# A two-part transformer kernel on one core: clamp, Newton step and entry normalizing made by GpSimd in place of VectorE, with a new merge order

## The chip, the cores and the metric

The program runs on 1 core of one Trainium2 chip. The metric is the device time of one execution, in microseconds (us). Engines are named as the profile names them: PE is TensorE's matmul row and PEld its weight load, DVE is VectorE, ACT is ScalarE, POOL is GpSimd, SP is SyncE, which only issues transfers here.

## The reference, cut to what matters

`x` has 8 batches of 512 rows of 128 features. Each batch goes through a modulated layer norm, an attention with 16 heads of 8 features over all positions, a gated residual, a second modulated layer norm, two layers of a block with local attention, and a last gated residual.

```python
h = _layernorm(x) * (1 + ca) + sa
x = x + ga * attention(h)                  # 16 heads
h = _layernorm(x) * (1 + cb) + sb
x = x + gb * block(h)                      # 2 layers of _layer

def _layer(x, ...):
    q, k, v = split(shift_token(x) @ wqkv)  # 8 heads of 64
    q, k = l2norm(q) * qs, l2norm(k) * ksc  # t / max(norm(t), 1e-12)
    q, k = rotary_xpos(q, k)
    x = x + local_attention(q, k, v) @ wo   # windows of 64, looking one back
    h = layernorm(shift_token(x)) * lg + lb
    a, g = split(h @ w1 + b1)
    return x + (a * gelu(g)) @ w2 + b2
```

## The kernel before, in words

The work is cut into four streams of steps. Stream `a` is the first attention of all 8 batches, one after another. Streams `x`, `y` and `z` are the two-layer block: stream `x` takes batches 0, 1, 2 and 5, `y` takes 3 and 6, `z` takes 4 and 7 (`BATCHES`). Stream `x` runs beside `a`; `y` and `z` begin when `a` is over, because they use its memory. Each engine has a generator for each stream that issues one step at a time, and `merge` takes the steps in the order of a string of letters that is written out for each engine (`ORDER`). A second string, `BANKS`, says which PSUM bank each step of PE writes. Engines run their queue strictly in this order and wait for one another by semaphores, so an instruction that waits holds all that stands behind it on its engine.

One stream and layer of the block ("a stream layer", 16 in all) goes like this. PE projects keys, values and queries of 4 row tiles. For each of the 8 tiles of keys and queries ACT squares (L970), DVE multiplies by the rotary tables (L1258, L1262) and sums the squares over each head (L1266), and POOL adds the two rotary products (L825). When the 4 key tiles are summed, and again for the 4 query tiles, the norm is made from sums of 128x32: DVE clamps and shifts them (`b_norm`, L1272), ACT takes logarithm and exponential (L978, L980) for a first inverse root, DVE improves it with a Newton step of three instructions (`b_rnorm`, which calls `newton`, L1148 to L1150), and POOL multiplies the four tiles by it (`b_scale`, L833). Then PE transposes (L530), and for each of 8 heads come scores (L541, L548), maximum on DVE (L1284), exponential on ACT (L998), reciprocal on DVE (L1289), weighing on POOL (`b_probs`, L838), transpose (L558) and product with the values (L569). The output projection (L579), a layer norm and a gated hidden layer (L598, L604) close the layer.

The rows that enter an attention are normalized by DVE. For the first attention `a_normalize` does a Newton step on 128x4 numbers and four `tensor_scalar` of 128x128 into `xn` (L1154). For each batch that enters the block `b_enter_normalize` does the same into `xn2`, which is memory of `rot_work`. PE then transposes them (L442, L516). The layer norm inside the block reads PSUM, is written to `work`, and is not touched by the change.

In the first attention, DVE takes a maximum (L1191), ACT an exponential (L905), DVE a reciprocal (L1195) and POOL weighs the queries (`a_weigh`, L803) for each of 16 groups of a batch. POOL also splits keys and values into two parts (`a_split`, L786, L788) and adds the residual (`a_residual`, L792).

Of the kernel before, what the change touches and what calls it, by code (L numbers as in the profile page):

```python
# [14 lines left out]
P = 128  # L15
# [50 lines left out]
B_CHAIN = LN_CHAIN + (2 * 2 + LN_CHAIN) * L  # L66
# [4 lines left out]
        "aaaaaaaaaaaaaaaaaaaaaaaaaaaaaaaaaaaaaaaaaaaaaaaaaaaaaaaaaaaaaaaaaaaaaaaaaaaaaaxaaaaaaaaaaaaaaaaaaaaa"  # L71
        "aaaaaaaaaaxaaxxxxxxaxaaxxaaaaaaaxxaaaaxxxxaaaaaaaaaaaaaaaxxxxaaaaaaaaaaaaaaaaaaaaaaaaaaaaaaaaaaaaaaa"
        "aaaaaaaaaaaaaaaaaaaaaaaaaaaaxxaaaxaaxaaaaaaaaaaaaaaaaaaaaaaaaaaaaaxxxaxaxxaaaxxaaaxaaaaxxaaaaaaxaaax"
        "aaaaaaxaaaaxaxaxaaaxxxxxaaaaaaxaaaaaxxaaxxxxaxxaxaaaaaaaaaaxxaaxxxaxaaaaaaaaaxxaxxaaaaxxaaaxxxxaxxxa"
        "aaxxxaaaxxxaaaaxaxaaaxaaaaaxxxxaaxaxaxaaxaaaaaaxaaaaaaaaaaaaaaxaaaxxxaxxxxxaaaaaxxaaaaaaaaaaaxaxaxxx"
        "xaaaaaaaaaxxxaaxaaaaxxaaaxxaaaxxxaxxaxxxaxxxxxyxyyyyyyyxyyxxxxxxyxyyxxxxxxxxxxyyyyxxxxxxyyyyxyxxxyxx"
        "yyyxxyxxxxxyxyxxyyxxxyyxxyyyxyyxxxxxxyxxyxyyyyyyxzyzzzzzzzzzzxxxxxxzzxxzzzzxxyyyyyyyyzzzzyzxxxxxxyzz"
        "zzzzzzxxxzzxzyyzzzxzxzxxxzxyxyyxxyzxxzzxzzzzxyzxxyzxzzxzzxzzzzzyyxyxxxxxxzzxzzzzyyxxxxxyxzzxyyyzxzxx"
        "zyyyyxxzzyyxyxxxyzzzyzzzyzzzxyxxxzzzxzxzyxxxzyyyyyyzxxyzzyzxxxzxzzyzyyzxxyxxyyyyxyzxzzzxzzyyzzzzxzxx"
        "xxxxyyxyyxyyzzzzzzxxxxzxzxzzxzyzyyyxxzyxzxyzzzyyzzxxzzyzyyxzzxzxyyzyyxzyyxyzyxxyxyzxzzzyxxzzzxzxyxxy"  # L80
        "xxzzzzzzzzyyxxxyyyxzxxyxzxyzzxzyzzzyyyyxyyyxxyxxzxxzzzxzzyyyyyyzxxxzxzzxxxzxyxyxyzzyyzzxxzyxxxxyyzyy"
        "yzxyxyxxyyzxxzyzxyyxxxxyzxyxyxxzyxzzzzzzyxxxyyxyxyyxyzyxzyxxxxxxxx"
    ),
    "DVE": (
        "aaaaaaaaaaaaaaaaaaaaaaaaaaaaaaaaaaaaaaaaaaaaaaaaaaaaaaaaaaaaaaaaaaaxaaaaaaxaaaaaaaaaaaaaaxaaaaaaaaaa"
        "aaaaaaaaaaaaaaxaaaxaaaxaaxxaxxaaaxaaaxaaaxaaaaaaaxaxaaaaaxaaaaaaaaaaaaaaaaaaaaaaaaaaaaaaaaaaaaaaaaaa"
        "aaaaaaaaaaaaaaaaaaaaaaaaaaxxaxxxxaaaaxaaaaaaaaaaaaaaaaaaaaaaaaaaaaaaxxxxaxxxaaaxxxaaaxaaaaaxaaaaaaax"
        "aaaxaxaaaaaxaxaaaaaaaaxxxxaaaxaaaaaaaxaxaaxaxaaxaxaaaaaxxaaaxaaxaaaxaaaxaaaaaaxaaaaxxaaaxxxxaxxxaaxx"
        "xxaxxxxaaaxxaaaxaaxxaaxaaxaaaaaxaxaaxaaxaaaaaaxaaaaaxaaaaaxaaaaxaaaxaaxxaaaaxaxaaxaaaaxxaaaaaaaxxaxa"
        "aaxaaaaaaxaaaaaxxaxxaaxxxaaaxxaxxxxxxxxaxyxyxxxyxyxyyyyyxxxyyxxyxxxxxxxxyxyyxxxyyyxyyxxyyyxxxxyxyxxx"  # L90
        "xxxxyyyxxxyyxxyyyxyxxyxyxyyxxyxyxxxzyxzyyxzyyzzzzzzzzxxzzxzxzxxxxyzyzzxzyyzzzxzyxyzzxyzzzyzzzzzxzyzx"
        "zxxxxxxzzxzxxxzxxxyyxxxyxzzzzzxzxzxxxzxzyzzzzxxxyzxyxyzyzyyyzxxxyxyyxzyyxzzxyzxyyyyxzzzyyzxxzzxyzzzz"
        "zyyzzzyzxzxxzyxxxxzxzxzxzyyyxxxyyyxxyzzzxxxyzxyzzxyzxyzyxyxzxzxyyzzyxxxzzxzzxxzxzyxzyzxyxyxzzzzzyzzx"
        "yxxyzyyzyyzzzxxyzzzzzyzxyzyyyzyyxzxyyyxyzzyzyxzyyxxxyxxxzzzyxzzxxxxxxxzzzzzxxxyyyxzxyyxzzxxyxzxzyzyz"
        "yxyyxxzyyxzzxzzyzzyzxyxzzyxzxzxxzzyzxxyyzzyzyyyxxyxyyxzyyzyyyxyyxxyzxxxxyzzxyxxxxxzyxzxyyxxxyxyzzzxx"
        "xxyyxyxzyzyxxxxx"
    ),
    "ACT": (
        "aaaaaaaaaaaaaaaaaaaaaaaaaaaaaaaaaaaaaaaaaaaaaaaaaaxaaaaaaxaaaaaaaaaaaaaaaaaaxaaxaaaxxxaxxxxaaxaxxaaa"
        "axxaaaxxxaaaaaxxaaaaxxxxaaaaaaaaaaaaaaaaaaaaaaaaaaaaaaaaaaaaaaaaaaaaaxxaxaxxaaaxaaaaaaaaaaaaaaaaaaxx"  # L100
        "xaxxaaxxaaxaaxaxaaaaaaxaaaaxaxaaaaxaaxaaaaxaaaxxaxxxxxxaxaxaaaaxxaaxxxaaaaxxaaaxxaxxaaaaxxaxaxxxxxax"
        "xxaxaxxaxaxaaaaxaxaxaaxaaaaaaaaaaaaxaaaxaxaaxxaxxxaxxxaaxaxaxaaaaxaaxaxxxaaxxaaaaxaxaxxaaaxxxxxxaaaa"
        "xxxxxxxxxxyyxyyxyyyyyxyyyxyyyxyxxxxxxxxxyxxyyxxxyxyxyxxyyyxxyxxyyxxxyyxxxyyxxxxxyxyxxyyxxyyyxyyxxyxy"
        "yyxzxxzzyzzzzzzzzzzxzxxxzzxxzxzzxyyxzzyyxxzzzzyyxyxzzxxxyyyzzzzxxyzzzzxxzzxzzxyyzzxxxxzxxxzxyxxyyzxx"
        "yyxzxyzxxyzzzxzzzxzzzyyxzzxzzyzxzzyyzxxxxyyxyxzzxzyzyxzxyxxyzzyxxyyyzxyxxzzyzxxzzzzzyzxzzxxxzzyxxxyz"
        "xxxxzyzxxzxyxxyyxyyxyxxzyyyyyzzzxzzzzxyyyzzzxxzzyyzyyyzzzxzzxxzzxxxzyxzyxzzxyzyyyzxxzzxzyzyyxxyyyzzz"
        "zzxzxzzyyzyzyxxxyyxxyyzxyyxxzxzyxxzyxxxxzyxxxxxzzzzzzzzyxxxzxxyzzyxzzzyzxzyyyyxyyzzyxyzzzyzxzyyyzyzx"
        "yxxzzzxyyxzxxzxyxyzyzxyxzzxyyxxxxyyyyxzzyyyyzxxxxxyzyxxyyxxxyxzxyxxxzxyxzxxyzyxxyxxxx"
    ),
# [32 lines left out]
def build(nc, x, wmod, wqkv1, wqkv, wo, w1, w2, cols_in, rows_in_, rotary, out):  # L142
    with ExitStack() as ctx:
# [3 lines left out]
        def sb(name, shape, dt=F32):  # L147
            return tensor_in(ctx, name, shape, dt)
# [29 lines left out]
        clamp = sb("clamp", [P, J, H])  # L178
# [77 lines left out]
        def qk_of(s, i, w):  # L256
# [17 lines left out]
        s_gcol, s_tables, s_clamp, s_qz, s_kzero = (  # L274
            sem(n) for n in ("s_gcol", "s_tables", "s_clamp", "s_qz", "s_kzero"))
# [5 lines left out]
        xn_ready = sem("xn_ready")  # L281
# [15 lines left out]
        xn2_ready = sems("xn2_ready")  # L297
# [4 lines left out]
        ss_all, ss_log, ss_rsqrt, rn_ready = sems("ss_all"), sems("ss_log"), sems("ss_rsqrt"), sems("rn_ready")  # L302
# [460 lines left out]
        def _(pool):  # L763
# [17 lines left out]
            pool.memset(clamp[:], SHIFT2).then_inc(s_clamp, 1)  # L781
# [26 lines left out]
            def a_stream():  # L808
                for b in range(B):
                    for g in range(NG):  # L810
                        if b and g == 1:
                            a_residual(b - 1)
                            yield
                        a_weigh(b, g)
                        yield
                        if b + 1 < B and g in (5, 7):
                            a_split(b + 1, (g - 5) // 2)
                            yield
                a_residual(B - 1)
                yield  # L820
# [21 lines left out]
            def b_stream(s):  # L842
                for k in range(len(BATCHES[s])):
                    for l in range(L):
                        for n in range(2 * J):
                            if (k, l, n) == (0, 0, 0):
                                enter_wait(pool, s, k)
# [616 lines left out]
```

## Time and profile before

| | before |
|---|---|
| median of 3 runs | 1196.69 us (1193.58 to 1197.32) |
| profiled execution, its own time | 1196.15 us |
| span of the profiled execution | 1194.3 us |
| PE, DVE busy | 997.0 us (83%), 949.4 us (79%) |
| ACT, POOL busy | 918.2 us (77%), 508.1 us (43%) |
| mean granted clock of TensorE | 0.948 of full speed |

The span is the time from the first to the last instruction in the profile; 1.85 us of the execution's own time lie around it. Busy time leaves out waits for semaphores. The last step of the first attention begins at 559.7 us, so the run has two halves: up to about 560 us stream `a` beside stream `x`, then `x`, `y` and `z` together.

### The profile page before, as it was taken

Reading aid. Unit: us, or ns where it says so; the run is one execution under the profiler, and the core shown is the slowest. Engines: PE = TensorE matmul, PEld = TensorE weight load, DVE = VectorE, ACT = ScalarE, POOL = GpSimd, SP = SyncE. Lnnn points to the kernel's source line nnn. Section 1 sums busy time; section 2 is a strip of 40 time slices with the busy share of each in tenths; the row PEclk is TensorE's granted clock in tenths of the full one; section 3 lists DMA queues with packets and bytes.
Section 4 is the critical chain, followed back from the end, with each engine's and each line's share of the span. In section 5 each row is a group of like instructions: output and inputs, shape, how many; then the busy total and the mean of one; then the engine's idle time right before and its main releaser. Section 6 shows DMA issues by size and latency. Waiting matters only on the chain. (4 is left out here: it accounts for less than half of the span.)

```text
span 1194.3 us, 23996 instructions
## 1 busy us (share of the span) xinstructions
PE 997.0 (83%) x8124; PEld 510.0 (43%) x8124; DVE 949.4 (79%) x1947; ACT 918.2 (77%) x2782; POOL 508.1 (43%) x578
## 2 busy tenths in 40 slices
PE   2677787768888798778868897899999789999898
PEld 2232232223323352234336444655664357545664
DVE  4789898888869777986884699779769976789865
ACT  1698979899978988887659566868886587958983
POOL 5012143212105321343474058647823676348830
PEclk8699989999989898998989998999999999999999
DMA  5541305232204103001011001101110020001200
GB/s 206 180 142 36 106 1 146 62 107 71 72 0 130 43 28 115 10 10 24 1 31 34 10 1 32 33 1 32 33 41 10 10 63 16 18 1 32 46 20 27
DMA packets 28009, 59.18 MB, mean 50 GB/s; under 512 B 6192, under 2 KB 6384, under 8 KB 26736
## 3 DMA queue, kind: packets, MB, share of 16 engines
q1 hardware_dynamic: 27120, 56.33, 16.7%
q8 instruction: 67, 1.10, 0.4%
q10 hardware_dynamic: 768, 1.31, 0.3%
q14 instruction: 54, 0.44, 0.1%
HBM read 23.98 MB, written 18.87 MB: 36 GB/s over the span
## 5 line engine op out<-in xcount | busy, mean ns | idle before, releaser
L905 ACT ACTIVATE E<-psum,neg_max 128x512 f32<-128x512 f32 x512 | 346.6, 716 | 64.2 <-DVE neg_max L1191 45.9
L1191 DVE TENSOR_REDUCE neg_max<-psum 128x2 f32<-128x1024 f32 x256 | 307.5, 1214 | 58.7 <-PE psum L465 56.7
L465 PE MATMUL psum<-v_rows,k_rows 64*128 64x512 f32 x512 | 130.3, 514 | 106.0 <-ACT E L905 79.6
L998 ACT ACTIVATE rot_work<-psum,neg 128x128 f32<-128x128 f32 x512 | 184.3, 412 | 17.9 <-DVE neg L1284 11.0
L838 POOL TENSOR_TENSOR rot_work<-rot_work,rz 128x512 f32<-128x512 f32 x128 | 133.0, 1047 | 141.0 <-DVE rz L1289 140.9
L825 POOL TENSOR_TENSOR work<-work,rot_work 128x512 f32<-128x512 f32 x96 | 121.7, 1273 | 129.6 <-DVE rot_work L1262 129.3
L465 PEld LDWEIGHTS psum<-v_rows,k_rows 64*128 64x128 f32 x512 | 52.8, 196 | 250.6 <-ACT E L905 116.1
L803 POOL TENSOR_TENSOR qz<-qT,rz 128x32 f32<-128x32 f32 x128 | 30.8, 241 | 300.7 <-DVE rz L1195 299.8
L523 PE MATMUL psum<-wqkv_sb,hs 128*128 128x512 f32 x288 | 144.0, 622 | 6.8 <-DVE hs L1248 3.8
L474 PE MATMUL psum<-E,qz 128*32 128x512 f32 x1024 | 148.2, 653 | 0.2 <-POOL qz L803 0.2
L998 ACT ACTIVATION_READ_ACCUMULATOR rot_work<-psum,neg 128x1 f32 x512 | 126.7, 252 | 0.0
L905 ACT ACTIVATION_READ_ACCUMULATOR E<-psum,neg_max 128x1 f32 x512 | 119.8, 234 | 0.0
L1284 DVE TENSOR_REDUCE neg<-psum 128x4 f32<-128x512 f32 x128 | 85.5, 677 | 36.2 <-PE psum L548 36.1
L833 POOL TENSOR_TENSOR work<-work,rn 128x512 f32<-128x512 f32 x96 | 99.6, 1056 | 16.6 <-DVE rn L1150 16.6
L970 ACT ACTIVATE rot_work<-psum 128x512 f32<-128x512 f32 x128 | 77.9, 612 | 31.0 <-PE psum L523 22.3
L598 PE MATMUL psum<-work,w_sb 128*128 128x512 f32 (+1 forms) x192 | 94.0, 623 | 2.7 <-ACT work L1013 2.1
L558 PE MATMUL psum<-ident,rot_work 128*128 128x128 f32 x512 | 80.8, 286 | 15.5 <-POOL rot_work L838 8.8
L1008 ACT ACTIVATE prT<-psum 128x512 f32<-128x512 f32 x128 | 79.2, 636 | 11.5 <-PE psum L569 8.2
L1262 DVE TENSOR_TENSOR rot_work<-psum,rot 128x512 f32<-128x512 f32 x128 | 87.0, 679 | 0.0
L1266 DVE TENSOR_REDUCE ss<-rot_work 128x8 f32<-128x512 f32 x128 | 86.4, 675 | 0.0
L558 PEld LDWEIGHTS psum<-ident,rot_work 128*128 128x128 f32 x512 | 57.1, 143 | 45.6 <-POOL rot_work L838 26.3
L1258 DVE TENSOR_TENSOR work<-psum,rot 128x512 f32<-128x512 f32 x96 | 65.4, 681 | 12.6 <-ACT rot_work L970 12.3
(140 smaller groups left out, 1784.7 us busy)
## 6 DMA issues: line engine op xcount, KB each, us to landing
k_rows<-k_scr SPq DMA_DIRECT2D x128, 64.0 KB, 1.9
work<-v_al SPq DMA_DIRECT2D x16, 512.0 KB, 4.4
v_rows<-v_scr SPq DMA_DIRECT2D x124, 64.0 KB, 1.9
work<-v_al SPq DMA_DIRECT2D x16, 384.0 KB, 5.7
k_scr<-hi SPq DMA_DIRECT2D x16, 256.0 KB, 3.0
k_scr<-lo SPq DMA_DIRECT2D x16, 256.0 KB, 3.3
v_scr<-hi SPq DMA_DIRECT2D x14, 256.0 KB, 2.9
v_scr<-lo SPq DMA_DIRECT2D x14, 256.0 KB, 3.1
```

What stands on the lines that cost most here:

```text
L465: pe.matmul(bank, k_rows[r:r + 64, half, hh, P * j:P * (j + 1)], v_rows[r:r + 64, b % 2, hh, :], start=True, stop=True).then_inc(full, 1)
L474: last = pe.matmul(O_BANK[32 * q:32 * q + 32, :], qz[:, hh, j % QZ_SLOTS, q, :], E[:, (b * NG + g) % E_RING, q, :], start=(g == 0), stop=( ...
L523: pe.matmul(bank, hs[s][:, P * i:P * (i + 1)], wqkv_sb[:, l, INNER * c:INNER * (c + 1)], start=True, stop=True).then_inc(full, 1)
L558: last = pe.transpose(bank[:, P * w:P * (w + 1)], pr[s][:, u % PR_SLOTS, w, :], ident[:])
L598: pe.matmul(bank[0:CH[c]], w1_sb[:, l, o:o + CH[c]], h2T[s], start=True, stop=True).then_inc(full, 1)
L825: pool.tensor_tensor(qk_of(s, i, w), qk_of(s, i, w), sinp[s][:, n % 2, :], ALU.add).then_inc(rot_sum[s], 1)
L833: pool.tensor_tensor(v, v, rn[s][:, i, w, :].unsqueeze(2).broadcast_to([P, H, DH]), ALU.mult).then_inc((q_ready, k_ready)[w][s], 1)
L838: pool.tensor_tensor(pr[s][:, u % PR_SLOTS], pr[s][:, u % PR_SLOTS], rz2[s][:, u, :].unsqueeze(2).broadcast_to([P, 4, 2 * W]), ALU.mult).t ...
L905: act.activation(E[:, (b * NG + g) % E_RING, 2 * half + m, :], pair[:, m], ACT.Exp, bias=neg_max[:, n, m:m + 1], accum_out=z[:, n, m:m + 1 ...
L998: last = act.activation(pr[s][:, u % PR_SLOTS, w, :], bank[:, 2 * W * w:2 * W * (w + 1)], ACT.Exp, bias=neg2[s][:, u, w:w + 1], accum_out= ...
L1191: dve.tensor_reduce(neg_max[:, n, :], pair, AX.X, ALU.max, negate=True).then_inc(max_ready, 1)
L1262: dve.tensor_tensor(sinp[s][:, n % 2, :].rearrange("p (h a r) -> p h a r", h=H, a=2), bank.rearrange("p (h a r) -> p h a r", h=H, a=2)[:, ...
```

## The change

Three pieces of DVE's work go to POOL. The clamp of `b_norm` becomes one `tensor_scalar` on POOL with two constants (the constant tile `clamp` and its memset go). The Newton step of `b_rnorm` becomes four POOL instructions, each waiting for the one in front of it. The `tensor_scalar` of 128x128 of the two entry normalizings go to POOL, four for each batch; DVE keeps their Newton step of 128x4, and POOL waits for it through new semaphores (`a_scale`, `x2_scale`). In POOL's stream of the block, a batch's normalizing is a step of its own ahead of the first rotary addition, and the two norms are steps after the 4th and 5th and after the 8th rotary addition. All five order strings and the bank string are written anew. Nothing else changes: PE's and ACT's instructions and all transfers are the same ones in another order.

```diff
-B_CHAIN = LN_CHAIN + (2 * 2 + LN_CHAIN) * L
+ENTER_CHAIN = 2 + 2
+B_CHAIN = ENTER_CHAIN + LN_CHAIN * L
...
 ORDER = {
     "PE": (
...
-        "yzxyxyxxyyzxxzyzxyyxxxxyzxyxyxxzyxzzzzzzyxxxyyxyxyyxyzyxzyxxxxxxxx"
...
+        "zyzzxzyzxzzyzyxyyzyyzxzyyyyxyyyxxyyyxxxyzxyyxyzyzzyzzzzzyzyyyyyyyy"
...
     "POOL": (
...
-        "xyxzzxxxxxyyzxxyyxxxxyzyyxxyxxxxxx"
...
+        "xyxzzzzzyyzyzzzzyyyzzyzyzzxzzxzxxxxxxxxxxxxxxxxxyxxyzzzzzzzyzyzzzzxzxzzxyzxzzzzyxxyyyzzzxxyyzzyyzyyz"
+        "yyyyzyyyyyyyy"
...
+            def normalize(dst, src, mv, rstd):
+                for j in range(J):
+                    last = pool.tensor_scalar(dst[:, j, :], src[:, j, :], mv[:, j, 0:1], rstd[:, j:j + 1],
+                                              ALU.subtract, ALU.mult)
+                return last
+
+            def a_normalize(b):
+                pool.wait_ge(a_scale, b + 1)
+                normalize(xn, x_sb[:, b], mv, rstd0).then_inc(xn_ready, 1)
+
+            def b_enter_normalize(s, k):
+                pool.wait_ge(x2_scale[s], k + 1)
+                normalize(xn2[s], x_sb[:, BATCHES[s][k]], mv1[s], rstd1[s]).then_inc(xn2_ready[s], 1)
...
+                        if b + 1 < B and g == 1:
+                            a_normalize(b + 1)
+                            yield
                         a_weigh(b, g)
...
+            def b_norm(s, k, l, w):
+                passed(pool, ss_ready[s], (k * L + l) * 2 * J + J * (2 - w))
+                v = ss[s][:, :, w, :]
+                pool.tensor_scalar(v, v, NORM_MIN2, SHIFT2, ALU.max, ALU.mult).then_inc(ss_all[s], 1)
+
+            def b_rnorm(s, k, l, w):
+                n = (k * L + l) * 2 + 1 - w
+                pool.wait_ge(ss_rsqrt[s], n + 1)
+                v, r, t = (a[s][:, :, w, :] for a in (ss, rn, nt))
+                pool.tensor_tensor(t, v, r, ALU.mult).then_inc(rn_chain[s], 1)
+                pool.wait_ge(rn_chain[s], 4 * n + 1)
+                pool.tensor_tensor(t, t, r, ALU.mult).then_inc(rn_chain[s], 1)
+                pool.wait_ge(rn_chain[s], 4 * n + 2)
+                pool.tensor_scalar(t, t, -0.5, 1.5, ALU.mult, ALU.add).then_inc(rn_chain[s], 1)
+                pool.wait_ge(rn_chain[s], 4 * n + 3)
+                pool.tensor_tensor(r, r, t, ALU.mult).then_inc(rn_chain[s], 1)
...
             def a_normalize(b):
                 dve.wait_ge(a_rstd, b + 1)
-                ln_link(newton(var_e[:], rstd0[:], tmp4[:], ln_link))
-                normalize(xn, x_sb[:, b], mv, rstd0).then_inc(xn_ready, 1)
+                newton(var_e[:], rstd0[:], tmp4[:], ln_link).then_inc(a_scale, 1)
                 ln_end()
...
-            def b_norm(s, k, l, w):
-                passed(dve, ss_ready[s], (k * L + l) * 2 * J + J * (2 - w))
-                v = ss[s][:, :, w, :]
-                dve.scalar_tensor_tensor(v, v, NORM_MIN2, clamp[:], ALU.max, ALU.mult).then_inc(ss_all[s], 1)
-
-            def b_rnorm(s, k, l, w):
-                dve.wait_ge(ss_rsqrt[s], (k * L + l) * 2 + 2 - w)
-                newton(ss[s][:, :, w, :], rn[s][:, :, w, :], nt[s][:, :, w, :], b_link_of(s, k)).then_inc(rn_ready[s], 1)
```

## Rows read from the trace of the kernel before

**Rows 1.** Busy time by stage: PE, PEld, DVE, ACT, POOL, then clock, DMA share, GB/s
```profile
50.00:560.00 510.00, 410.14 (x2780) 164.96 (x2772) 426.42 (x739) 445.72 (x1331) 142.97 (x231) 0.93 0.23 66
560.00:640.00 80.00, 61.54 (x460) 34.56 (x461) 59.00 (x131) 49.68 (x146) 46.55 (x42) 0.94 0.10 24
640.00:1140.00 500.00, 457.73 (x4417) 272.02 (x4416) 404.75 (x928) 376.48 (x1192) 294.21 (x267) 0.98 0.10 24
1140.00:1195.00 55.00, 49.42 (x408) 28.25 (x406) 33.19 (x91) 31.60 (x81) 6.25 (x6) 0.98 0.04 16
```

**Rows 2.** The chain that ended last, by engine, as shares of the span
```profile
PE 23%; DVE 15%; ACT 3%; issue 3%; POOL 2%; DVEq 0%; ACTq 0%
```

**Rows 3.** Busy time in single stretches of 10 us, columns as in rows 1
```profile
590.00:600.00 10.00, 9.23 (x24) 3.78 (x24) 9.25 (x16) 6.05 (x11) 9.03 (x9) 1.00 0.00 0
600.00:610.00 10.00, 6.09 (x29) 3.30 (x28) 9.90 (x19) 4.64 (x10) 7.43 (x7) 1.00 0.00 0
...
740.00:750.00 10.00, 5.49 (x117) 4.21 (x116) 9.86 (x21) 7.08 (x33) 8.75 (x9) 1.00 0.01 2
...
1110.00:1120.00 10.00, 9.44 (x140) 6.71 (x132) 9.53 (x20) 8.35 (x38) 9.49 (x10) 1.00 0.41 94
1120.00:1130.00 10.00, 8.32 (x166) 6.92 (x165) 7.56 (x17) 9.97 (x44) 9.65 (x11) 1.00 0.01 3
```

**Rows 4.** Groups of VectorE's instructions from 560 us on: busy, mean ns
```profile
L1272 DVE SCALAR_TENSOR_TENSOR ss<-ss,clamp 128x32 f32<-128x32 f32 x26 | 17.2, 666 | 0.3
L1149 DVE TENSOR_TENSOR nt<-nt,rn 128x32 f32<-128x32 f32 x26 | 14.1, 543 | 0.9
L1148 DVE SCALAR_TENSOR_TENSOR nt<-ss,rn 128x32 f32<-128x32 f32 x26 | 12.3, 472 | 2.9 <-ACT rn L980 2.8
...
L1150 DVE SCALAR_TENSOR_TENSOR rn<-nt,rn 128x32 f32<-128x32 f32 x26 | 7.3, 281 | 0.9
L1154 DVE TENSOR_SCALAR rot_work<-x_sb,mv,rstd 128x128 f32<-128x128 f32 x24 | 6.7, 343 | 0.2
```

**Rows 5.** Two of the moved groups on VectorE from 50 to 560 us
```profile
L1154 DVE TENSOR_SCALAR xn<-x_sb,mv,rstd 128x128 f32<-128x128 f32 x24 | 6.7, 342 | 0.2
L1272 DVE SCALAR_TENSOR_TENSOR ss<-ss,clamp 128x32 f32<-128x32 f32 x6 | 2.1, 352 | 0.2
```

**Rows 6.** Duration of one instruction in ns, least/median/most, whole run
```profile
L1272 DVE SCALAR_TENSOR_TENSOR ss<-ss,clamp x32: 159/744/1278, 159.6 to 1121.3; 128x32 f32<-128x32 f32 x32
L1149 DVE TENSOR_TENSOR nt<-nt,rn x32: 191/193/1185, 164.2 to 1123.6; 128x32 f32<-128x32 f32 x32
```

**Rows 7.** Groups of GpSimd's instructions, whole run
```profile
L803 POOL TENSOR_TENSOR qz<-qT,rz 128x32 f32<-128x32 f32 x128 | 30.8, 241 | 300.7 <-DVE rz L1195 299.8 <-PE psum L474 0.9
L788 POOL TENSOR_TENSOR lo<-kf,hi 128x512 fp32r<-128x512 f32 x16 | 20.5, 1283 | 1.3
L871 POOL TENSOR_TENSOR rot<-rot,rows 128x128 f32<-128x128 f32 x8 | 3.5, 454 | 0.0
L769 POOL CAST ident_h<-ident 128x128 bf16<-128x128 f32 x1 | 0.3, 291 | 0.1
```

**Rows 8.** The chain in order of time, first and last moved piece: start, us
```profile
685.68 1.11 DVE rot_work L1154 x4
...
1111.32 0.03 DVE rn L1150
```

**Rows 9.** GpSimd in order of time: start, us, instruction, idle before
```profile
942.94 3.50 POOL L833 TENSOR_TENSOR work<-work,rn 128x512 f32<-128x512 f32 x3
...
1124.88 2.04 POOL L833 TENSOR_TENSOR prT<-prT,rn 128x512 f32<-128x512 f32 x2 [0.35 <-DVE rn L1150]
...
1157.45 1.04 POOL L838 TENSOR_TENSOR rot_work<-rot_work,rz 128x512 f32<-128x512 f32 x1 [0.67 <-DVE rz L1289]
```

**Rows 10.** Who waited for whom from 50 to 560 us: total, times, longest
```profile
ACT E L905 <- DVE neg_max L1191: 25.3, 32, 2.0
```

More of the change, by code:

```diff
@@ new lines @@
+        "aaaaaaaaaaaaaaaaaaaaaaaaaaaaaaaaaaaaaaaaaaaaaaaaaaaaaaaaaaaaaaaaaaaaaaaaaaaaaaaaxaaaaaaaaaaaaaaaaaaa"
+        "aaaaaaaaaxaxxxxxxaaaxxxaaaaaaaaaaaxxxxxxaaaaaaaaaaaaaaaaaxxxaaaxaaaaaaaaaaaaaaaaaaaaaaaaaaaaaaaaaaaa"
+        "aaaaaaaaaaaaaaaaaaaaaaaaaaaaxxaaaxaaxaaaaaaaaaaaaaaaaaaaaaaaaaaaaxxxaxxaxaxxaxaaaxxaaaaaxaxaaaaaxaaa"
+        "aaxaxxxxxxaaaxaaaaxxxxxxaaaxxxaaaaaxaaaaaaaxaaxaaxxaaaaaxxaaaaaaaxxxxaaaaaaaaxaaaaaaaaaxxaaaxaxxxxxa"
+        "aaxxxaaaxaaaaxaaaxaaaxaaaxaaaaaxaaaaaxaxxxxxxaaaxaaaxaaaaaaaxaaaaaxaxxxxxaaxaxxaaxaaaaaaaxxaaxxaxxaa"
@@ L97 @@
+        "zzxxzxzxxxyzzyzyyxzyzyyyxzzzzzyzyyyxyxxxxxxyxyzzxxxxyxyyxxxxxyxxyzxzzzxxzzzyxzxyzzyzzzyzzyxxzxzzzxzx"
+        "xzxzzyyyzxzxxyxxxxzzzyyzyxxzyzyzyyyyxzyxxzxxzxxzxzzzyyxxxzxxxxxxxzxxyyyxyyyyyxxyxyxyzyyzzyyzyyxxxzzz"
+        "yzxxyzyzzzzxyzzyyzzzxzyxzyzxxxzzyyyzzxyxyzzzyzzyzzzzzyyxzxxxxzxxzxxxxxyyxxxzzzxxzxzzzxyzzxzzzzyzzxzz"
+        "zxzxzxyxyyzyyyyzyzyyyyyyyyyyxxxzyxzyyxyyyzzzyzzyyyyy"
     ),
     "ACT": (
[L99 removed]
@@ L273, in build @@
         s_silexp, s_sil, s_setup = sem("s_silexp"), sem("s_sil"), sem("s_setup")
-        s_gcol, s_tables, s_clamp, s_qz, s_kzero = (
-            sem(n) for n in ("s_gcol", "s_tables", "s_clamp", "s_qz", "s_kzero"))
+        s_gcol, s_tables, s_qz, s_kzero = (
+            sem(n) for n in ("s_gcol", "s_tables", "s_qz", "s_kzero"))
         s_chain = sem("s_chain")
@@ L843, in b_stream @@
                 for k in range(len(BATCHES[s])):
+                    enter_wait(pool, s, k)
+                    b_enter_normalize(s, k)
+                    yield
                     for l in range(L):
                         for n in range(2 * J):
-                            if (k, l, n) == (0, 0, 0):
-                                enter_wait(pool, s, k)
                             b_rotary(s, k, l, n)
                             yield
+                            if n == J - 1:
+                                b_norm(s, k, l, 1)
+                                yield
+                            if n == J:
+                                b_rnorm(s, k, l, 1)
+                                yield
                             for i in {J: (0,), J + 1: range(1, J)}.get(n, ()):
@@ L852, in b_stream @@
                                 yield
+                        b_norm(s, k, l, 0)
+                        yield
+                        b_rnorm(s, k, l, 0)
+                        yield
                         for i in range(J):
@@ L858, in b_stream @@
                             yield
+            a_normalize(0)
             a_split(0, 0)
```

116 lines of the change are left out of this document (47 added, 69 removed).

## The prediction, made before the changed kernel was timed

> **What bounds the kernel now.** I read the busy time by stage first [rows 1], because the two halves of the run have different limits. Up to 560 us ACT is the fullest engine, 445.7 of 510 us, with DVE close behind at 426.4. From 560 us to the end (635 us) the four figures add up to PE 568.7 us (90%), DVE 496.9 (78%), ACT 457.8 (72%) and POOL 347.0 (55%). So the mean names PE as the bound of the second half, and POOL as the engine with room.
>
> The chain of work that ended last says something else [rows 2]. It can be followed back to 638 us, and in these 556 us PE holds 23% of the span, DVE 15% and POOL 2%. An engine that is busy 78% of the time still owns about a third of the chain, so there must be stretches where DVE is the limit. The stretches of 10 us show them [rows 3]. Of the 63 stretches between 560 and 1190 us, 18 have DVE at 9.5 us or more; the first is at 600 us, the last at 1110 us. In these 18 PE is idle for 21.7 us in sum, as 3.9 us at 600 and 4.5 us at 740. There are 9 stretches with POOL at 9.0 or more, the first at 590 and the last at 1120, and there PE is idle 14.8 us in sum; three of them (720, 1100 and 1110) are among the 18 as well. These are the stretches of rotary products and norms, where streams do that part of their layer at the same time.
>
> **What leaves DVE.** From 560 us on, 26 of the 32 norms are made. Their clamp costs 17.2 us and the three Newton instructions 14.1, 12.3 and 7.3 us, the entry normalizing of 6 batches 6.7 us [rows 4]: 57.6 us, or 11.6% of DVE's work there. Before 560 us it is less: 6.7 us for `xn`, 2.1 us for 6 clamps [rows 5], some 3.6 us for their 18 Newton instructions at about 0.2 us, and about 2.2 us for 8 entry instructions at the price of rows 4: 14.6 us.
>
> The durations are worth a look. A clamp of 32 columns takes 159 ns at best and 1278 ns at most, and its median is 744; the second Newton instruction takes 191 to 1185 ns [rows 6]. Nothing in the instruction varies. The most is the length of one of POOL's additions, 1283 ns [rows 7]. So these instructions, which read two tensors from SBUF, are mostly held while POOL works on a tile. At their best the second half's 26 norms would cost 26 x (0.159 + 3 x 0.19) = 19 us in place of 50.9; the other 32 us are being held.
>
> The Trainium skill says this of the hardware: in SBUF — State Buffer, section "Who interferes with whom", a VectorE instruction with two SBUF inputs contends with a GpSimd instruction that reads SBUF, and the one that comes second waits for all of the other. The trace agrees with it, as far as VectorE being held goes. By that page alone the move would take 50.9 us off DVE and not the 19 us that the free durations give; rows 4 already say so.
>
> **What it costs on POOL.** The two-input instruction of 128x32 is there: 241 ns [rows 7]. POOL's form with one input and constants isn't. For 128x128, the one-input cast takes 291 ns and the two-input product 454 ns [rows 7]; the new `tensor_scalar` has one tensor input, so I take 0.29 us, with 0.45 as the upper end. For 128x32 I take 0.21 us from the same slope, with 0.24 as the upper end and nothing below the 0.1 us or so of an empty instruction. A wait of one POOL instruction for the one before it costs 1.3/16 = 0.08 us (L788 waits so for L786) [rows 7]. A norm on POOL is thus 0.21 for the clamp and 3 x 0.24 + 0.21 + 3 x 0.08 = 1.17 us for the Newton step. On DVE the same step takes 1.30 us in the second half (rows 4, mean values), so the latency of the norm hardly changes; the hop from DVE to POOL, 0.35 us [rows 9], stands in front of the clamp in place of in front of the scaling.
>
> From 560 us on POOL gains 26 x 1.38 + 24 x 0.29 = 42.9 us and would be 390 us or 61% busy. In the whole run it gains 32 x 1.38 + 64 x 0.29 = 62.7 us, 7.7 us of it waits between its instructions.
>
> The Trainium skill speaks against such a move: GPSIMD Engine Reference, section "4.1 Engine selection", wants elementwise work on VectorE, with GpSimd about twice as slow for two inputs. Twice the free 0.73 us of a norm would be about 1.5 us as an estimate, near my 1.38; by that page the 26 norms turn 19 us of DVE into 38 us of POOL. The trace differs on the first of these numbers, since DVE in fact pays 1.96 us a norm.
>
> **What of it lies on the path.** I went through the chain piece by piece. The moved instructions appear in it as 59 pieces, the first at 685.68 us and the last at 1111.32 [rows 8]: 6.3 us of clamps, 11.8 us of Newton instructions, 4.6 us of entry normalizing, 22.7 us together. That is 39% of their 57.6 us, about the share that DVE's work as a whole has (15% of the span is 180 us, of 497). POOL's own pieces in the chain are 2% of the span [rows 2], 24 us of 347, or 7%. The added 42.9 us of POOL at 7% are 3 us. They fall mostly into the rotary stretches, where POOL is fullest, so I double that to 6 us and add 1 us for hops. This gives -22.7 + 7 = -16 us. If a piece leaves the chain, the next slower engine takes over, and PE is right behind at 90%; what PE can give back in the stretches where DVE is full is 21.7 us in all [rows 3]. I take a quarter off: -12 us.
>
> In the first half ACT sets the pace and waits 25.3 us for DVE's maxima [rows 10]. Of 14.6 us taken off DVE, I count a fifth: -3 us; the ends are 0 and the 39% of above, -6. The POOL work added there is covered: POOL is idle 300.7 us in front of `a_weigh` alone [rows 7], and each batch's normalizing is issued ahead of the second weighing, when that still waits for a reciprocal. If the cover were gone, 7 batches x 1.2 us = 8 us would be lost. The head of the run has one `a_normalize` more on POOL, whose memsets are over by then: 4 x 0.29 us in place of 1.1 us, nothing.
>
> **The new order** I can only read, not price by rows. The stream `x` has 127 steps on PE before the last step of `a` in the old string and 124 in the new one, so the halves are cut alike. The end differs. Before, stream `x` ends last; when its last scores begin, 55 of PE's steps are left, 27 its own and 28 of the others. In the new string stream `y` ends last, with 48 steps left, 21 of the others. POOL's string also ends with 8 weighings of `y` and nothing beside them. Since PE has 997 us for 1166 steps, 7 steps fewer are 6 us of cover less. The end after the last weighing takes 36 us now (1158.5 to 1194.3) [rows 9], and PE is 90% busy from 1140 us [rows 1]. I take +3 us, between 0 and +6.
>
> The sum is -12 - 3 + 3 = -12 us. Against the profiled execution's own 1196.15 us that is 1184 us, and its own time is within 0.6 us of the median 1196.69, so I predict 1184.
>
> **Rivals.**
>
> *The gain is larger.* All of PE's idle time in DVE's 18 full stretches comes back, 21.7 us, the first half gives its 6, the end costs nothing: -28 us, 1168 us. For it speaks that 32 us of DVE's time were pure holding; against it, that PE's own work stays.
>
> *Hidden.* PE at 90% takes over wherever DVE lets go, and the new order's end eats the rest: within 3.6 us of before, 1193 to 1200. Speaking for it: in 13 of DVE's 18 full stretches PE is busy 9 us or more too. Against it: the chain still goes through DVE there.
>
> *POOL becomes the limit in the rotary stretches.* For one stream and layer POOL has 8 additions of 1.27 and 8 scalings of 1.05 us, 18.5 us, against DVE's 8 x 2.03 = 16.3 us without the norms. The norms make it 21.3 us. `b_rnorm` waits on POOL for ACT's exponential, and behind it stand additions and weighings of the other streams, on which DVE's next products (two buffers) and PE's transposes depend. If in the stretches where POOL is at 9.0 or more each norm lies on the path with its hop, about a third of the 26, 9 x (1.38 + 0.35) = 16 us come on; when more than 60% of the norms do so, 16 x 1.73 = 28 us, it outweighs the 22.7 us that leave. With the waits for ACT, of which DVE now has 2.8 us [rows 4] and POOL could have several times that, I price it at +10 us: 1207 us. Against it speaks that POOL has only 7% of its time in the chain.
>
> *The lock turns round.* POOL's small instructions may themselves be held by DVE, as one scaling seems to be, 3.50 us for three in place of 3.1 [rows 9]. The Trainium skill, Perfetto Trace Analysis, section "Optimizing Scalar/DVE Operations", warns that offloading between these two might not help since they share a port. If each of POOL's 160 new norm instructions lost as much as DVE's four do now, 0.3 us, it would be 48 us on POOL, and at 7 to 14% of the path 3 to 7 us: 1189 us. It is a smaller gain, not a loss; I count it with the forecast.
>
> **Chances.** The forecast with its spread, 1174 to 1192: 0.55. Larger gain: 0.13. Hidden: 0.14. POOL the limit or an order that ends badly: 0.18. Faster by over 0.3% (3.6 us, about what a measurement of this kernel tells from no change) is 0.68, within it 0.14, slower 0.18. The range goes from 1163 to 1202: the low end takes in the larger gain with 5 us for an order that packs better than I can see, the high end takes in the hidden case and the weaker half of the slower one.
>
> **What the profile of the changed kernel would show.** DVE's busy time at about 875 us (949.4 less 57.6 and 14.6, and about 2.5 before 50 us) and POOL's at about 563. The clamp on POOL at 0.2 to 0.25 us each with no spread; the 128x128 instructions at 0.3 to 0.45. Fewer than 18 stretches with DVE above 9.5. The chain with less than 15% on DVE, and POOL at 3 to 4%. Wrong would be: POOL's instructions with spreads up to a microsecond (the lock turned round), POOL at 8% or more of the chain with waits of POOL for ACT's L980 of over 10 us in sum (the third rival), DVE stretches as full as before (an order that just shifts work), or a span after the last weighing of more than 40 us (a bad end). A first half that ends after 565 us would speak against the cover of POOL's work there.

## The result, and the profile after

The changed kernel takes 1200.65 us (median of 20 runs, 1197.24 to 1206.09); the kernel before, run beside it, takes 1195.41 us (20 runs, 1191.32 to 1198.19). The ratio is 1.0046, with a 95% interval of 1.0035 to 1.0058: slower by about 5.5 us, where 12 us less were forecast. The profiled execution is one of the longer ones, 1205.59 us with a span of 1203.8 us, so about 4 of the 9.4 us between the two profiled executions are spread between runs (it lies 4.9 us above its median, the profiled execution of before 0.7 above its own), and I read its shares and durations rather than its total.

The busy line and the line of engines in the chain that ended last, from the page of the changed kernel, answer to the table of before and to [rows 2]:

```profile
PE 1001.6 (83%) x8124; PEld 518.9 (43%) x8124; DVE 890.0 (74%) x1755; ACT 920.1 (76%) x2782; POOL 598.9 (50%) x801
...
PE 43%; DVE 24%; POOL 13%; ACT 11%; issue 5%; SPq 2%; DMA 1%; ACTq 0%; DVEq 0%; POOLq 0%
```

DVE lost 59 us. POOL gained 91, not the 55 that I had added up. The shares of the two chains can't be set side by side as they stand, because the chain of before reaches back only to 638 us and this one to the start. Summed from 638 us on, POOL's pieces grew from 24.6 to 99.2 us (8% of the whole span, to be held against 2%) and DVE's shrank from 177 to 100.

Busy time by stage in the changed kernel, columns as in [rows 1]:

```profile
50.00:560.00 510.00, 410.59 (x2749) 166.54 (x2748) 414.30 (x683) 446.03 (x1326) 174.54 (x293) 0.93 0.24 68
560.00:640.00 80.00, 60.58 (x345) 33.09 (x347) 48.60 (x104) 42.39 (x107) 51.14 (x63) 0.85 0.05 12
640.00:1140.00 500.00, 455.82 (x4471) 275.21 (x4468) 367.41 (x819) 378.53 (x1205) 333.43 (x390) 0.98 0.10 24
1140.00:1204.00 64.00, 57.62 (x509) 33.75 (x507) 38.13 (x101) 40.34 (x116) 15.73 (x18) 0.97 0.10 28
```

The first attention ends where it did (the first instruction of its last step, DVE's product with the gate, begins at 559.8 us, before at 559.7), though DVE has 12 us less to do there: POOL has 32 us more. And from 560 us on there are fewer stretches of 10 us that DVE fills and more that POOL fills. Two of the latter, to be held against [rows 3]:

```profile
750.00:760.00 10.00, 9.50 (x110) 6.51 (x105) 8.07 (x18) 9.34 (x40) 9.75 (x14) 1.00 0.01 2
...
980.00:990.00 10.00, 6.23 (x64) 4.38 (x66) 6.07 (x13) 6.69 (x25) 9.59 (x14) 0.83 0.01 2
```

Counted over all stretches, those with DVE at 9.5 us or more went from 19 to 11, and PE's idle time in them from 22.1 to 6.4 us. Those with POOL at 9.0 or more went from 9 to 16, and PE's idle time in them from 14.8 to 27.0 us. That looks as if PE now waited for POOL where it had waited for DVE, but the count alone doesn't show it. In the fastest kernel of the experiments below (e7) there are 17 stretches with POOL at 9.0 or more, with 28.6 us of PE's idle time in them, and in e1, which takes 2.1% longer than before, there are 3, with 3.0 us.

The groups of POOL's moved instructions, with busy time and mean ns of one, say why it is so much:

```profile
L795 POOL TENSOR_SCALAR rot_work<-x_sb,mv,rstd 128x128 f32<-128x128 f32 x32 | 25.3, 803 | 23.7 <-DVE rstd L1195 23.7
L795 POOL TENSOR_SCALAR xn<-x_sb,mv,rstd 128x128 f32<-128x128 f32 x32 | 25.3, 801 | 8.2 <-DVE rstd L1195 8.2
...
L847 POOL TENSOR_SCALAR ss<-ss 128x32 f32<-128x32 f32 x32 | 10.4, 324 | 2.7
...
L855 POOL TENSOR_TENSOR nt<-nt,rn 128x32 f32<-128x32 f32 x32 | 8.2, 255 | 2.5
L853 POOL TENSOR_TENSOR nt<-ss,rn 128x32 f32<-128x32 f32 x32 | 8.1, 254 | 12.5 <-ACT rn L1025 12.3
L859 POOL TENSOR_TENSOR rn<-rn,nt 128x32 f32<-128x32 f32 x32 | 8.1, 253 | 2.7
L857 POOL TENSOR_SCALAR nt<-nt 128x32 f32<-128x32 f32 x32 | 7.0, 218 | 2.8
```

The norms cost 41.8 us of busy time, where I had 36.5. The entry normalizing costs 50.6 us, where I had 18.6: a `tensor_scalar` of 128x128 that takes a mean and a scale per partition from memory runs for 0.80 us on POOL, against 0.34 on DVE. A batch's rows take 3.1 us. The timeline shows what that does in the first attention (start, duration, instruction, idle before):

```profile
96.81 3.13 POOL L795 TENSOR_SCALAR xn<-x_sb,mv,rstd 128x128 f32<-128x128 f32 x4 [0.52 <-DVE rstd L1195]
...
97.76 0.17 DVE L1239 RECIPROCAL rz<-z 128x4 f32<-128x4 f32 x1
...
99.91 0.24 POOL L816 TENSOR_TENSOR qz<-qT,rz 128x32 f32<-128x32 f32 x1
...
100.76 1.07 PE L474 MATMUL psum<-E,qz 128*32 128x512 f32 x8
```

The reciprocal is ready at 97.9 us. The weighing that needs it stands behind the normalizing in POOL's queue and starts at 99.9, 2.0 us late. So it is in five of the batches. But this delay is hardly what the run pays for: in the whole chain that ended last, these weighings (L816) hold 1.3 us. The normalizing itself holds 30.3 of its 50.6 us there, because PE's transposes (L442, L516) need the rows that it writes. Two pieces of that chain in order of time (start, us):

```profile
906.99 3.15 POOL rot_work L795 x4
...
910.19 0.66 PE psum L516 x4
```

PE's transposes waited 11.1 us in sum for L795, and before 6.3 us for the same rows made by DVE. The norms hold 13.9 of their 41.8 us in this chain.

### The profile page after: what moved, and what is told of

Same layout as the page of the kernel before. It is cut to its first block, busy times and chain, and to the rows that moved or that the text cites. A ratio compares the mean times of both kernels' runs of the same rounds, so it can differ in the third digit from the quotient of the medians.

```text
span 1203.8 us, 24023 instructions
## 1 busy us (share of the span) xinstructions
PE 1001.6 (83%) x8124; PEld 518.9 (43%) x8124; DVE 890.0 (74%) x1755; ACT 920.1 (76%) x2782; POOL 598.9 (50%) x801
## 4 chain that ended last, share of the span: by engine, by line
PE 43%; DVE 24%; POOL 13%; ACT 11%; issue 5%; SPq 2%; DMA 1%; ACTq 0%; DVEq 0%; POOLq 0%
DVE neg_max L1235 8%; PE psum L523 5%; PE psum L598 5%; PE psum L474 5%; ACT E L950 5%; PE psum L569 5%; PE psum L465 4%; PE psum L579 4%; PE psum L558 3%; PE psum L548 3%; ACT rot_work L1043 3%; PE psum L604 2%; DVE rot_work L1305 2%; POOL work L841 2%; POOL work L866 2%
## 5 line engine op out<-in xcount | busy, mean ns | idle before, releaser
L841 POOL TENSOR_TENSOR work<-work,rot_work 128x512 f32<-128x512 f32 x96 | 122.2, 1278 | 98.5 <-DVE rot_work L1305 97.9
L816 POOL TENSOR_TENSOR qz<-qT,rz 128x32 f32<-128x32 f32 x128 | 30.9, 241 | 266.4 <-DVE rz L1239 262.6
L1043 ACT ACTIVATION_READ_ACCUMULATOR rot_work<-psum,neg 128x1 f32 x512 | 121.7, 240 | 0.0
L866 POOL TENSOR_TENSOR work<-work,rn 128x512 f32<-128x512 f32 x96 | 99.9, 1058 | 1.0
L1053 ACT ACTIVATE prT<-psum 128x512 f32<-128x512 f32 x128 | 78.4, 623 | 20.2 <-PE psum L569 10.9
L598 PE MATMUL psum<-work,w_sb 128*128 128x512 f32 (+1 forms) x192 | 89.9, 609 | 3.0 <-ACT work L1058 2.8
```

The lines of the kernel that those rows point to most:

```text
L598: pe.matmul(bank[0:CH[c]], w1_sb[:, l, o:o + CH[c]], h2T[s], start=True, stop=True).then_inc(full, 1)
L841: pool.tensor_tensor(qk_of(s, i, w), qk_of(s, i, w), sinp[s][:, n % 2, :], ALU.add).then_inc(rot_sum[s], 1)
L866: pool.tensor_tensor(v, v, rn[s][:, i, w, :].unsqueeze(2).broadcast_to([P, H, DH]), ALU.mult).then_inc((q_ready, k_ready)[w][s], 1)
L1043: last = act.activation(pr[s][:, u % PR_SLOTS, w, :], bank[:, 2 * W * w:2 * W * (w + 1)], ACT.Exp, bias=neg2[s][:, u, w:w + 1], accum_out= ...
```

## The experiments

All ratios are against the kernel before, timed on the same chip, with 95% intervals. A kernel is called by the first part of its label (e1 to e12). Two theories are about where the loss comes from on POOL: A1, the entry normalizing and its 0.80 us; A2, the norms in the rotary stretches. Theory B is that the new order itself is worse.

**The order and the placement apart.** The first kernel keeps the new strings and puts everything back on DVE; the second keeps the old strings and puts everything on POOL. Since a string has a letter for each step, steps were taken out or put in at the place where the other engine began them in the profile. The edits are shown here and below cut to a few lines, this one in outline.

```diff
# new order, all on DVE: b_norm, b_rnorm and both normalize on dve as before
-            b_norm(s, k, l, 1)      # in pool's b_stream
+            b_norm(s, k, l, 1)      # in dve's b_stream, letters put into ORDER["DVE"]
```

> The new order strings and bank string with all three moved pieces back on DVE (in DVE's string each norm step stands where GpSimd began it in the changed kernel's profile). Theory A, GpSimd's longer queue is the cause of the loss: without it the new order is no worse than the old one, so 0.998 to 1.002 of before (1193 to 1198 us). Theory B, the new order itself packs worse and the moved work gains a little: as slow as the changed kernel or slower, 1.004 to 1.012.

> The old order strings and bank string with all three pieces on GpSimd (its steps put into GpSimd's string where DVE began them in the profile of before). Theory A: GpSimd's 599 us of work hurt in this order too, and it was not planned for them: 1.004 to 1.015 of before. Theory B: the old order with the work moved is faster than before, 0.985 to 0.997.

Measured: 1.0213 (1.0188 to 1.0239) for the new order with all on DVE, 1.0131 (1.0108 to 1.0155) for the old order with all on POOL. Both are slower than either of the two kernels in which order and placement belong together. The second result lies in the range of theory A, the first above the range of either theory. Theory A as I had put it, that the new order would be neutral, is wrong, and so is the B of the old order gaining by the move. How much of the two losses comes from the places at which the steps were inserted is not known, since no second set of places was run. The chain of the second kernel, of which the part from about 640 us can be followed, has the same engines as [rows 2] in other shares:

```profile
PE 23%; POOL 13%; DVE 6%; ACT 2%; issue 2%; POOLq 0%; DVEq 0%; ACTq 0%
```

DVE's 15% of before are 6%, and POOL's 2% are 13%: in this order the two engines changed places on the path.

**One piece at a time, in the new order.**

```diff
# norms back on DVE, normalizing stays on POOL: e3
-                pool.tensor_scalar(v, v, NORM_MIN2, SHIFT2, ALU.max, ALU.mult).then_inc(ss_all[s], 1)
+                dve.scalar_tensor_tensor(v, v, NORM_MIN2, clamp[:], ALU.max, ALU.mult).then_inc(ss_all[s], 1)
...
# normalizing back on DVE, norms stay on POOL: e4
-                newton(var1[s][:], rstd1[s][:], tmp1[s][:], link).then_inc(x2_scale[s], 1)
+                link(newton(var1[s][:], rstd1[s][:], tmp1[s][:], link))
+                normalize(xn2[s], x_sb[:, BATCHES[s][k]], mv1[s], rstd1[s]).then_inc(xn2_ready[s], 1)
```

> The changed kernel with clamp and Newton step back on DVE; the normalizing of the entering rows stays on GpSimd, 64 instructions of 0.80 us. Theory A1, the entry normalizing with its unforeseen 0.80 us is what costs: still slow, 1.003 to 1.008 of before. Theory A2, the norms on GpSimd are what costs: 0.996 to 1.001. Theory B: 1.004 or more.

> The changed kernel with the normalizing of the entering rows back on DVE (0.34 us an instruction in place of 0.80, and one hop less); the norms stay on GpSimd. Theory A1: the loss goes, 0.995 to 1.001 of before. Theory A2: it stays, 1.003 to 1.006. Theory B: 1.004 or more.

Measured: 1.0278 (1.0252 to 1.0303) with the norms back on DVE, 1.0008 (0.9993 to 1.0024) with the normalizing back. The first is outside what any theory gave: taking the norms off POOL makes the new order much worse, so A2 does not hold for it. The second fits A1. The norms may sit on POOL; the entry normalizing, in this form, costs when it does. POOL's share of the chain in that kernel falls from 13% to 8%:

```profile
PE 44%; DVE 27%; ACT 11%; POOL 8%; issue 5%; SPq 2%; DMA 2%; ACTq 0%; DVEq 0%; POOLq 0%
```

**One piece at a time, in the old order.** The edits are the same, with the strings of before.

> The old order with clamp and Newton step on GpSimd, entry normalizing on DVE. If GpSimd's queue in the rotary stretches is a cost of its own in any order (theory A2): 1.004 to 1.010 of before. If an order is only good for the placement it was made for, and the entry normalizing carries most of the old order's 1.0131 with everything on GpSimd (theory A1): 0.998 to 1.004.

> The old order with only the normalizing of the entering rows on GpSimd. Undoing it in the new order gave 0.0038 of the time back, 4.5 us. If that price (GpSimd 3.1 us a batch in place of 1.1, and a hop) holds in any order: 1.003 to 1.008 of before. If it was a matter of the new order: 0.999 to 1.002.

Measured: 1.0050 (1.0032 to 1.0068) with the norms on POOL, 1.0055 (1.0037 to 1.0073) with the normalizing there. The first lies in the range that I had given to theory A2, not in that of A1: in the old order the norms do cost. The second is as A1 has it. The price of the normalizing holds in both orders: 0.0055 alone and 0.0081 on top of the norms in the old one (1.0131 less 1.0050), 0.0038 and 0.0065 in the new one (1.0046 less 1.0008, 1.0278 less 1.0213). The norms on POOL cost 0.0050 in the old order and save 0.0205 in the new one (1.0213 less 1.0008), which was planned with them on POOL. How much of this is queue length and how much the place of my inserted steps is not told apart.

**The instruction's form.** If 0.80 us an instruction is the fault, another form of the same arithmetic on the same engine must help. Rows of before had a POOL product of 128x512 with a broadcast operand at 1.05 us.

```diff
             def normalize(dst, src, mv, rstd):
-                for j in range(J):
-                    last = pool.tensor_scalar(dst[:, j, :], src[:, j, :], mv[:, j, 0:1], rstd[:, j:j + 1],
-                                              ALU.subtract, ALU.mult)
-                return last
+                entered[0] += 1
+                pool.tensor_tensor(dst[:], src, mv[:, :, 0:1].broadcast_to([P, J, D]),
+                                   ALU.subtract).then_inc(nz_chain, 1)
+                pool.wait_ge(nz_chain, entered[0])
+                return pool.tensor_tensor(dst[:], dst[:], rstd[:].unsqueeze(2).broadcast_to([P, J, D]), ALU.mult)
```

> The changed kernel; the four tensor_scalar of 128x128 with scalars from memory are replaced on GpSimd by one subtraction and one product of 128x512 with the scalars as a broadcast operand. Such a product took 1.05 us in the profile of before, so a batch costs 2.2 us in place of 3.1. If the duration of the entry normalizing is what costs (theory A1), about 0.9 of the 2 us a batch come back, 0.998 to 1.004 of before, and below the changed kernel's 1.0046. If its place in GpSimd's queue costs and not its length: as the changed kernel, 1.004 to 1.006. If an instruction with broadcast scalars is slow on GpSimd as well, slower.

Measured: 0.9945 (0.9929 to 0.9961), 1190.88 us. This is below every range that I had given: I had expected 0.9 us back for each batch and at best 0.998. With nothing else changed the kernel goes from slower than before to faster than before, and this is the fastest kernel of the study. It is also faster than e4, which has the normalizing on DVE. Its groups and, from its timeline, the same place of the first attention as above:

```profile
L800 POOL TENSOR_TENSOR rot_work<-rot_work,rstd 128x512 f32<-128x512 f32 x8 | 8.4, 1049 | 0.6
L797 POOL TENSOR_TENSOR xn<-x_sb,mv 128x512 f32<-128x512 f32 x8 | 8.3, 1044 | 7.8 <-DVE rstd L1198 7.8
```

```profile
96.00 1.04 POOL L797 TENSOR_TENSOR xn<-x_sb,mv 128x512 f32<-128x512 f32 x1 [0.49 <-DVE rstd L1198]
...
97.12 1.04 POOL L800 TENSOR_TENSOR xn<-xn,rstd 128x512 f32<-128x512 f32 x1
...
98.12 0.24 POOL L819 TENSOR_TENSOR qz<-qT,rz 128x32 f32<-128x32 f32 x1
...
99.97 1.06 PE L474 MATMUL psum<-E,qz 128*32 128x512 f32 x8
```

The weighing starts 2.1 us after the normalizing began, and not 3.1. Yet PE's product with the values starts 3.97 us after it, and 3.95 us in the changed kernel: at this place the earlier weighing buys PE nothing. What changed is the normalizing's own part of the chain. It holds 8.5 us there in place of 30.3, and PE's transposes waited 5.0 us for it in place of 11.1. POOL's whole time for it is 33.3 us in place of 50.6.

One thing more differs between the two profiles. Of their 14.8 us of span, PE's idle time makes only 5.3; for 9.5 us PE is busy longer with the same 8124 matmuls (1001.6 against 992.1 us), at a mean granted clock of 0.941 against 0.953. Over all runs the median clock is 0.941 in the changed kernel and 0.9465 in e7, so part of the gain may come by way of the clock. Whether it does, and how large the part is, stays open: the other five runs of e7, at 0.946 to 0.950, take no longer than the profiled one, within their spread, and the kernel before had a median of 0.951 beside e7 and is slower all the same.

**Which half, and is it the time or the form?** Two kernels use the wide form in one half only. A third keeps the wide form and makes its subtraction twice, into the same place with the same values, so that a batch is as long on POOL as in the changed kernel.

```diff
# the subtraction made twice
+                for _ in range(2):
+                    entered[0] += 1
                     pool.tensor_tensor(dst[:], src, mv[:, :, 0:1].broadcast_to([P, J, D]),
                                        ALU.subtract).then_inc(nz_chain, 1)
                     pool.wait_ge(nz_chain, entered[0])
```

> New order, all on GpSimd; the entry normalizing of the first attention in the wide form (2.1 us a batch), that of the block still by four tensor_scalar (3.1 us). The profiles put the end of the first attention at 559.8 us in the changed kernel and 551.8 us with the wide form, and the rest at 644 and 637 us. If the first attention carries the gain of the wide form (1.0046 to 0.9945), this is near the wide kernel: 0.994 to 0.999. If the block does: 1.001 to 1.005.

> The counterpart: the first attention by four tensor_scalar, the block in the wide form. If the first attention carries the gain: 1.001 to 1.005. If the block does: 0.994 to 0.999. If each carries its part, both kernels lie near 0.9995.

> The wide form with its subtraction made twice (same values), so that a batch takes 3.2 us on GpSimd as in the changed kernel, but without its slow instruction. If it is the time on GpSimd that costs, it is as slow as the changed kernel: 1.003 to 1.007. If the four tensor_scalar do harm in another way, by holding DVE or by their form, it stays near the wide kernel: 0.995 to 0.999.

Measured: wide in the first attention alone 1.0002 (0.9990 to 1.0013), in the block alone 0.9995 (0.9986 to 1.0004), made longer 1.0071 (1.0052 to 1.0090). The two halves give about half of the gain each, as the third case of the expectations has it. The two single profiles had said about the same: 8.0 of their 14.8 us lie before the end of the first attention. The longer wide form is as bad as the changed kernel or a little worse; its batch takes 3 x 1.05 + 2 x 0.08 = 3.3 us against 3.1. So what costs is the time that the normalizing takes on POOL, and not some harm that the slow instruction does to others: its rows are 32.5 us of the chain again, and DVE is busy for as long in all three kernels (890.0 us in the changed one, 891.8 in e7, 891.6 here), so it isn't held more either. From 2.2 to 3.3 us a batch, 16 batches have 17.6 us more and the time rises by 0.0126, or 15 us: 0.86 us of the run for each microsecond of entry normalizing, whatever the clock's part in it (its median is 0.942 here and 0.9465 in e7).

**The old order with the wide form.**

> The old order with everything on GpSimd, entry normalizing in the wide form; with four tensor_scalar it was 1.0131. If the instruction's length costs as it did in the new order (0.0101), this is 1.001 to 1.006; if that was particular to the new order, 1.009 to 1.013. Either way the old order does not get below 1.000 with this placement, if an order only fits its own.

Measured: 1.0060 (1.0046 to 1.0073), 0.0071 below its counterpart with four `tensor_scalar`. The instruction's length costs in this order as well, a little less. The range for that case was 1.001 to 1.006. PE's transposes waited 19.2 us for the normalizing in e2 and 10.9 us here.

**What holds DVE's clamp.** One line of the kernel before:

```diff
-                dve.scalar_tensor_tensor(v, v, NORM_MIN2, clamp[:], ALU.max, ALU.mult).then_inc(ss_all[s], 1)
+                dve.tensor_scalar(v, v, NORM_MIN2, SHIFT2, ALU.max, ALU.mult).then_inc(ss_all[s], 1)
```

> The kernel of before with one line changed: DVE's clamp takes its factor as a constant and not from a tile, so it reads one tensor from SBUF. If the second SBUF input is what holds it while GpSimd works, its mean falls from 0.607 us to 0.16 to 0.25 us, DVE loses 11 to 14 us of busy time, and with 39% of that on the path the time is 0.995 to 0.999 of before. If DVE is held in this form too, its mean stays above 0.4 us and the time is the same, 0.999 to 1.001.

Measured: 0.9982 (0.9965 to 1.0000), which is not clearly different from before, and the mechanism that it was made for did not hold: the clamp's mean is 0.597 us, where it was 0.607, and DVE's busy time 948.0 us, where it was 949.4. Least, median and most ns of the clamp in that kernel:

```profile
L1272 DVE TENSOR_SCALAR ss<-ss x32: 150/736/1265, 158.9 to 1118.4; 128x32 f32<-128x32 f32 x32
```

With one SBUF input it is held just as in [rows 6]. A second input is not needed for it.

The placements and orders in one table, ratios to before:

| placement | old order | new order |
|---|---|---|
| all on DVE | 1 | 1.0213 |
| norms on POOL | 1.0050 | 1.0008 |
| entry normalizing on POOL | 1.0055 | 1.0278 |
| all on POOL (the change) | 1.0131 | 1.0046 |
| all on POOL, wide form | 1.0060 | 0.9945 |

## Why the prediction was wrong, point by point

**The step that failed** is in "What it costs on POOL": "the new `tensor_scalar` has one tensor input, so I take 0.29 us, with 0.45 as the upper end". It measured 0.80 us. The term "64 x 0.29 = 18.6 us" was 50.6 us, and even the upper end, 29 us, was far below. I had ranked the unknown instruction by its number of tensor inputs and paid no heed to its form, with a mean and a scale from memory for each partition (why it takes 0.80 us, no run shows); nothing in the trace of before had that form on POOL, so neither row bounded it from above. The nearest row was DVE's own use of the same form, 0.34 us for 128x128, double what DVE's free instruction of 32 columns takes. It was a hint that this form is dear.

**The weight of that term** failed with it, and it is what turned the sign. With 0.80 us in place of 0.29 my own sum would have moved by a microsecond or two: "The added 42.9 us of POOL at 7% are 3 us" would have become 55.1 us at 7%, doubled 8 us in place of 6, and in the first half the work was taken as covered. From e7 to e12 a microsecond of entry normalizing costs 0.86 us of the run, and in the chain of the changed kernel it holds 60% of its time (30.3 of 50.6 us), against the 7% and the double of it that I counted in the block and the nothing in the first attention.

**The cover** was the next step to fall. I had written that in the first half the POOL work is covered, since POOL is idle 300.7 us in front of the weighings, and that without the cover 8 us would be lost. The idle time is real, but e10, which leaves only the first attention with the long form, gives up 0.0050 of the time to e7; there was no full cover. Two things happen. The weighing behind the normalizing starts 2.0 us late in five batches, but PE's product after it starts at most 0.9 us earlier in e7, where the delay is 1.0 us, and in two of the five no earlier. And PE's transposes need the normalized rows: in the first attention the normalizing holds 12.1 us of the chain, in four of the eight batches. One of them is the first, for which I had put "nothing": its rows take 3.15 us on POOL in place of 1.11 on DVE, with nothing to hide behind. A sum of idle time on POOL says that POOL can take the work, and nothing on who waits for the result. The sign that I had named, a first half that ends after 565 us, did not show it: it ends at 559.8. In one profile each, it ends at 559.6 us in e4, without this work on POOL, and at 555.4 in e12, with the longest form, so the end of the first half is too uncertain a sign.

**The mechanism of the gain** was right in its first part. DVE's stretches at the limit lost 15.7 us of PE's idle time, of the 22.1 that I had as the bound (I had counted 18 stretches and 21.7 us; the one at 580 us belongs to them as well). That this is where a gain comes from is not shown: in e7, the kernel that gains, they lost only 7.8 us (10 stretches, 14.3 us). DVE's busy time fell to 890 us, where I had 875: some remaining instructions take longer beside the fuller POOL, as DVE's 128x4 products, 162 ns before in the mean, at 212, and its shift copies of 64x511, 517 ns before, at 626. These two make 4.2 of the 15 us; the rest was not traced. With the entry normalizing at 2.2 us a batch the same change gives 0.9945, that is -6.6 us against my -12. With the 1.2 us a batch that I had assumed, going on along the slope of e7 and e12 would give some 13 us more, as an estimate; no kernel here shows that, and no form that fast was found on POOL.

**POOL's weight on the path.** "At 7% are 3 us, doubled to 6": POOL's share of the chain did not stay what it was. Of 351 us of POOL's work from 638 us on, 99 us are in the chain, over a quarter; before it was 24.6 of 300 us, 8%. A share read from a trace holds for the schedule in it; an engine that is not on the path gets there once it is given more, and then all its work weighs more, not only the added part.

**The rivals.** The third one, POOL as the limit of the rotary stretches, is the nearest to what happened: its sign was POOL at 8% or more of the chain. The page has 13%, but over the stretch that the chain of before covers it is 8%, just at the sign. The waits for ACT's inverse root came to 12.3 us, just over the 10 that I had named. But its cause was put in the wrong place. I blamed the norms; e4 shows that with the norms alone on POOL the new order is level with before, and that the normalizing makes the difference. Its price was +10 us, the measured loss 5.5, and since the price was built from the norms, that they lie so close is luck. The lock turned round was not seen: POOL's clamp takes 319 to 382 ns in all 32 cases. What was lengthened was DVE.

**The order.** I gave it +3 us and said that I could not price it by rows. For it I had counted 6 us of cover less at the end and ends of 0 to +6. The end did not show this: from the start of the last weighing it is 31.8 us (1172.0 to 1203.8), and before it was 36.9. And e1 shows how much there was elsewhere: the new strings with the old placement cost 2.1%, 25 us. They are no reshuffling of equal worth but belong to this placement, as far as the places of the inserted steps allow to say so. The price of a placement in the old order and the price of the new order can't be combined either: 1.0131 x 1.0213 would be 1.035, and the changed kernel is 1.0046. My sum took the work out of the old schedule and left this out. With placement fixed I can't say whether a better string exists for e7.

**The hold of DVE by POOL** is real (19 us free against 50.9), but my reading that it comes from two SBUF inputs was too narrow, as e8 shows. The Trainium skill, in SBUF — State Buffer, section "Who interferes with whom", names beside the two inputs also `tensor_scalar` and copies in a mode that uses two ports. The run agrees with it so far: the one-input clamp had a median of 736 ns. Which mode it ran in no row shows. I had quoted only the half of that rule that the row seemed to show.

## What to carry to other kernels

Before work is moved to another engine, measure its exact instruction form there, with scalars from memory or constants; the number of tensor inputs does not tell its price. An engine's idle time tells that it can take a piece, and not that the piece is covered: ask who needs its result and when, and what stands behind it in the queue. And where the order is written out by hand or by a planner, placement and order are one thing: the old order took 1.3% and the new one 2.1% longer than before with the other's placement, so test a placement with an order made for it and then correct the piece that the plan priced wrongly.

## What the runs showed of the hardware that was not expected

A `tensor_scalar` of 128x128 on GpSimd with subtract and multiply and both scalars from memory takes 796 ns in the median (790 to 955), against 342 ns on VectorE; the same rows by two `tensor_tensor` of 128x512 with broadcast operands 2.1 us a batch against 3.1. For constants it is cheap: 218 ns for 128x32 with multiply and add, but 319 ns with maximum and multiply. VectorE's `tensor_scalar` of 128x32 with constants takes 150 ns at least and 1265 at most, as widely spread as the form with two SBUF inputs (159 to 1278), so one SBUF input does not keep an instruction free of the hold.
